# The low half of z made once per chunk and kept in DRAM; the down bias copied into the bank by ScalarE

## The reference

```
layer 0, per batch:
  q, k, v = x @ Wq, x @ Wk, x @ Wv;  attn = softmax(q k^T * 512**-0.5)
  a   = attn @ v @ Wp + bp
  cms = gelu(a @ cW1 + cb1) @ cW2 + cb2 + onehot(target)
  mod = gelu([a, cms] @ mW1 + mb1) @ mW2 + mb2
  z   = clip(x + cms + mod, 0, 1)
layer 1, per batch, with the weights of the batch's role (3 roles):
  h = gelu(z @ W_down[role] + b_down[role])          512 -> 256
  y = z + h @ W_up[role] + b_up[role]                256 -> 512
  out = layernorm(y) * gamma[role] + beta[role]
```

## Time and profile before

| | |
|---|---|
| time of the profiled execution | 2032.4 us |
| its span | 2030.8 us |
| median of three runs | 2033.6 us |
| busy: TensorE, weight load, VectorE, ScalarE | 2005.9, 1670.6, 1391.9, 950.2 us |
| mean granted TensorE clock | 0.998 |
| DMA of the whole program | 193.8 MB |
| last stage | from 1895 us on |
| store of 1 MB of z from POOL's queue, issue to landing | 5.1 us (median) |
| load of 128 KB of z, issue to landing | 2.1 us (median) |
| first half of `output` on VectorE, L1411 | 0.42 us |
| one clip, L1446 or L1457 | 0.42 us |
| DMA rate from 1894 to 1906 us | 374 to 430 GB/s |

### The profile page before, as it was taken

The page is one execution under the profiler, slowest core; times in us unless marked ns, Lnnn a source line. Parts: engine busy times, 40 slices in busy tenths (PEclk is TensorE's granted clock), DMA queues, the critical chain, the costliest instruction groups (busy, mean ns, idle before and its releaser), DMA issues.

```text
span 2030.8 us, 28039 instructions
## 1 busy us (share of the span) xinstructions
PE 2005.9 (99%) x9371; PEld 1670.6 (82%) x9371; DVE 1391.9 (69%) x2601; ACT 950.2 (47%) x1977; POOL 107.4 (5%) x199
## 2 busy tenths in 40 slices
PE   8999999999999999999999999999999999999997
PEld 7888878888888888888888888888888888888896
DVE  6786786555777686556686786565686686654897
ACT  4754453433654454333564453343374454433564
POOL 0000000000000000000000000000000000000132
PEclk9999999999999999999999999999999999999999
DMA  4121233315111143125111232224311132222754
GB/s 167 32 63 42 75 123 109 94 52 202 63 52 63 52 145 109 50 90 206 65 53 48 68 116 97 89 94 152 118 35 60 53 114 99 94 74 75 247 162 116
DMA packets 113024, 193.79 MB, mean 95 GB/s; under 512 B 12393, under 2 KB 72050, under 8 KB 108404
## 3 DMA queue, kind: packets, MB, share of 16 engines
q1 hardware_dynamic: 98404, 128.42, 20.1%
q0 software_dynamic: 14400, 63.46, 8.9%
q10 hardware_dynamic: 80, 0.13, 0.0%
HBM read 148.71 MB, written 43.26 MB: 95 GB/s over the span
## 4 chain that ended last, share of the span: by engine, by line
PE 91%; DVE 5%; DMA 2%; issue 1%; SPq 1%; ACT 0%; DVEq 0%; POOL 0%; POOLq 0%
PE y L1712 16%; PE y L1714 15%; PE y L1713 15%; PE x L1712 13%; PE x L1714 13%; PE x L1713 13%; PE y L1801 1%; PE x L1826 1%; DVE w_lo L1145 1%; DMA bet<-beta 1%; DVE c_forms L1307 1%; DMA w_blocks<-w1m 1%; PE x L2062 1%; DVE f L1211 0%; PE y L1800 0%
## 5 line engine op out<-in xcount | busy, mean ns | idle before, releaser
L693 ACT CAST w_hi<-w_blocks 128x512 fp32r<-128x512 f32 (+1 forms) x464 | 231.4, 519 | 124.6 <-PE y L1714 83.7
L1145 DVE TENSOR_TENSOR w_lo<-w_blocks,w_hi 128x512 fp32r<-128x512 f32 (+1 forms) x464 | 249.9, 564 | 54.7 <-ACT w_hi L693 54.7
L1712 PE MATMUL x<-h_hi,w_hi 128*128 128x512 f32 x512 | 199.7, 390 | 0.0
L1712 PE MATMUL y<-h_hi,w_hi 128*128 128x512 f32 x512 | 199.4, 389 | 0.0
L1713 PE MATMUL x<-h_lo,w_hi 128*128 128x512 f32 x512 | 199.3, 389 | 0.0
L1713 PE MATMUL y<-h_lo,w_hi 128*128 128x512 f32 x512 | 199.2, 389 | 0.0
L1714 PE MATMUL y<-h_hi,w_lo 128*128 128x512 f32 x512 | 199.2, 389 | 0.0
L1714 PE MATMUL x<-h_hi,w_lo 128*128 128x512 f32 x512 | 199.2, 389 | 0.0
L1712 PE MATMUL y<-a_forms,w_hi 128*128 128x512 f32 x480 | 187.9, 391 | 2.1 <-DVE f L1248 2.0
L1714 PE MATMUL y<-a_forms,w_lo 128*128 128x512 f32 x480 | 186.9, 389 | 0.0
L1713 PE MATMUL y<-a_forms,w_hi 128*128 128x512 f32 x480 | 186.8, 389 | 0.0
(11 more groups left out here) (240 smaller groups left out, 4243.2 us busy)
## 6 DMA issues: line engine op xcount, KB each, us to landing
w_blocks<-w1m SPq DMA_DIRECT2D x128, 256.0 KB, 4.5
w_blocks<-w1c SPq DMA_DIRECT2D x64, 256.0 KB, 3.2
w_st<-w2c SPq DMA_DIRECT2D x64, 256.0 KB, 3.1
w_st<-w2m SPq DMA_DIRECT2D x64, 256.0 KB, 4.7
x_hi_lo<-x_halves POOLq DMA_DIRECT2D x6, 2048.0 KB, 11.0
zs<-z_by_batch SPq DMA_DIRECT2D x66, 128.0 KB, 2.1
cms<-f SPq DMA_DIRECT2D x32, 256.0 KB, 2.8
z_cms<-cms POOLq DMA_DIRECT2D x8, 1024.0 KB, 7.0
```

The source lines that it names most:

```text
L693: nc.scalar.copy(w1_hi[:, w % RING, cols], src).then_inc(w1_hi_s, 1)
L1145: nc.vector.tensor_tensor(w1_lo[:, w % RING, cols], src, f32(w1_hi[:, w % RING, cols]), ALU.subtract).then_inc(w1_lo_s, 1)
L1712: nc.tensor.matmul(ps, w[0], x[0], start=first, stop=False, skip_group_check=more)
```

## The change

In each chunk of 512 values of finished z (8 chunks per super-tile), ScalarE copies the high half into `pre_hi` and VectorE subtracts it from z and writes the low half, one word in four, so that in the tile a token's four chunks lie together ("by token"). That tile (`x_st`, in the last stage `zr` and `zc`) is stored beside z in `z_dram`, and each load of the last stage brings both. The stationary operand of the low x high product is then read out of the loaded slot with a step of four words, and the split of z on VectorE is gone. ScalarE's split keeps its work. The down bias is loaded to all partitions by one DMA, and ScalarE copies its row into the PSUM bank two pairs ahead; the products add to it. The bias matmul, its ones, its zeroed tile and its pass through DRAM are gone. VectorE's calls of `z_chunk_lo` stand in the turns where ScalarE's calls of `z_chunk_hi` stand.

```diff
-PRE_W = (1, 1, 1, 1, 1, 1, 1, 0)
+PRE_W = (1, 1, 1, 1, 1, 1, 0, 0)
...
-    z_dram = nc.dram_tensor("z_by_batch", (B, P, DC * S), F32).ap()
+    z_dram = nc.dram_tensor("z_and_low_half", (B, P, 2, DC * S), F32).ap()
...
-            z_hi, z_lo = hl("z", [P, 2, DC, P], at_l1)
-            brow = sb("brow", [P, R, KD], F32R, at_l1)
+            z_hi = sb("z_hi", [P, 2, DC, P], F32R, at_l1)
+
+            zs = sb("zs", [P, 4, 2, 2, DC * S], F32R, at_l1)
+            brow = sb("brow", [P, R, KD], on=at_l1)
...
+        def low_tile(s, t):
+            tile = x_st if s + 1 < NS else (zr, zc)[t]
+            return tile[:].rearrange("p c n -> p (c n)").rearrange("p (b s c) -> p b s c", b=BT, c=DC)
...
@@ sync: load_z @@
                 if n >= 4:
-                    sp.wait_ge(zl_s, n - 3)
+                    sp.wait_ge(d_mm, n - 3)
                     sp.wait_ge(zf_s, n - 3)
                 for k, b in enumerate(batches_):
-                    sp.dma_start(zs[:, slot, k, :, :].rearrange("p c s -> p (c s)"),
-                                 z_dram[bass.ds(b, 1)].rearrange("o p f -> (o p) f")).then_inc(zl[slot], 16)
+                    sp.dma_start(f32(zs[:, slot, :, k]),
+                                 z_dram[bass.ds(b, 1)].rearrange("o p h f -> (o p) h f")).then_inc(zl[slot], 16)
...
-            sp.wait_ge(brow_zero, 1)
-            sp.dma_start(f32(brow[0:2]).rearrange("p r n -> p (r n)"), bd_dram).then_inc(row_in, 16)
+            sp.dma_start(brow[:], bd.to_broadcast([P, R, KD])).then_inc(row_in, 16)
...
+                if m == 4 + DC:
+                    sp.wait_ge(zl_c, 2 * DC * NS - DC)
+                    store_z(NT - 2, zr, last_stored[0], 1)
...
+                if m == 6 + 2 * DC:
+                    sp.wait_ge(zl_c, 2 * DC * NS)
+                    store_z(NT - 1, zc, last_stored[1], 1)
...
@@ gpsimd, start of super-tile s @@
                 if s:
+                    pool.wait_ge(zl_c, 2 * DC * s - DC)
+                    store_z(2 * s - 2, x_st, zl_stored, 1)
                     pool.wait_ge(z2_ready, DC * s)
                     store_z(2 * s - 1, h1_tile, z2_stored)
+                    pool.wait_ge(zl_c, 2 * DC * s)
+                    store_z(2 * s - 1, x_st, zl_stored, 1)
...
-                    pass_down_bias(2 * DC * s + 2 * R)
...
-                    nc.gpsimd.memset(f32(brow[:]), 0.0).then_inc(brow_zero, 1)
...
@@ scalar: gelu_plain, form_a @@
+                    act.wait_ge(zl_c, 2 * DC * s)
...
+                if s and k == P6 and h == 0:
+                    act.wait_ge(zl_stored, 32 * s)
...
+            def z_chunk_hi(s, t, c):
+
+                n = 2 * DC * s + DC * t + c
+                act.wait_ge((z1_ready, z2_ready)[t], DC * s + c + 1)
+                if n % (2 * DC) == 0:
+                    act.wait_ge(pre_stored, 32 * (2 * DC * (s + 1) if s + 1 < NS else 2 * DC * s + 2 * R))
+                if n:
+                    act.wait_ge(zl_c, n)
+                nc.scalar.copy(pre_hi[:].rearrange("p (b s) -> p b s", b=BT), (zb1, zb2)[t][:, :, c, :]).then_inc(zh_c, 1)
...
@@ scalar: attention @@
                 query(s, DC + 2)
+                if s:
+                    z_chunk_hi(s - 1, 0, 0)
                 split_a(s, 7)
+                if s:
+                    z_chunk_hi(s - 1, 0, 1)
                 query(s, DC + 3)
                 split_v(m0)
+                if s:
+                    z_chunk_hi(s - 1, 0, 2)
...
+                    if s and p == 2:
+                        z_chunk_hi(s - 1, 1, 0)
                     normalise_p(m + 1)
                     split_v(m + 1)
+                    if s and p < 5 and p != 1:
+                        z_chunk_hi(s - 1, *((0, 3) if p == 0 else (1, p - 1)))
...
@@ scalar: last stage @@
-                src = zs[:, slot].rearrange("p k c s -> p c k s")
+                src = f32(zs[:, slot, 0]).rearrange("p k (c s) -> p c k s", c=DC)
...
+            def down_bias(n):
+                if n == 0:
+                    act.wait_ge(row_in, 16)
+                r = act.value_load(role_t[0:1, n:n + 1], min_val=0, max_val=R - 1)
+                if n < 2:
+                    act.wait_ge(part_s, 8 * NQ * NS - 3 + n)
+                else:
+                    act.wait_ge(hgelu_s, n - 1)
+                nc.scalar.copy(d_ps[n % 2][:, 0:KD], brow[:, bass.ds(r, 1), :].rearrange("p o n -> p (o n)")
+                               ).then_inc(bias_s, 1)
...
                     gelu_pair(n + 1, (u + 1) % 2)
+                    if n + 3 < NPAIR:
+                        down_bias(n + 3)
...
                 unit(n, n, n + 2 < NPAIR, n + 1 < NPAIR)
+                if 4 <= n < 4 + DC:
+                    z_chunk_hi(NS - 1, 0, n - 4)
+                elif 9 <= n < 9 + DC:
+                    z_chunk_hi(NS - 1, 1, n - 9)
...
@@ vector @@
+            def z_chunk_lo(s, t, c):
+
+                last, n = s + 1 == NS, 2 * DC * s + DC * t + c
+                if c == 0 and last:
+                    dve.wait_ge((z1_ready, z2_s)[t], DC * NS)
+                elif c == 0:
+                    dve.wait_ge(*((zl_stored, 32 * s + 16) if t else (prod[P6], (2 * NQ - 1) * (s + 1))))
+                dve.wait_ge(zh_c, n + 1)
+                nc.vector.tensor_tensor(low_tile(s, t)[:, :, :, c].bitcast(F32R), (zb1, zb2)[t][:, :, c, :],
+                                        batches(f32(pre_hi[:])), ALU.subtract).then_inc(zl_c, 1)
...
                 inverse(m0 + 1)
                 if s:
+                    z_chunk_lo(s - 1, 0, 0)
                     z2_sum(s - 1, 2)
                 query(s, DC + 3)
                 if s:
                     z2_sum(s - 1, 3)
+                    z_chunk_lo(s - 1, 0, 1)
                 split_v(m0)
+                if s:
+                    z_chunk_lo(s - 1, 0, 2)
...
-                if z:
-                    split_z(n + 2, u + 2)
...
@@ tensor: down @@
-                pe.wait_ge(zl_s, n + 1)
-                if n < 2:
-                    pe.wait_ge(part_s, 8 * NQ * NS - 3 + n)
+                pe.wait_ge(zh_s, n + 1)
+                pe.wait_ge(bias_s, n + 1)
                 ps = d_ps[u % 2][:, 0:KD]
-                nc.tensor.matmul(ps, ones2[:], rows(brow[:], r), start=True, stop=False)
+                low = zs[:, u % 4, 1].rearrange("p k (s c) -> p (k s) c", c=DC)
                 for k in range(DC):
                     w = [rows(half[:, :, k, :], r) for half in (wd_hi, wd_lo)]
-                    ins = mm3(ps, (z_hi[:, u % 2, k, :], z_lo[:, u % 2, k, :]), w, False, k == DC - 1)
+                    ins = mm3(ps, (z_hi[:, u % 2, k, :], low[:, :, k]), w, False, k == DC - 1, True)
```

More of the change, by code:

```diff
@@ L451, in _, with store_z @@
                             sp.dma_start(cf_dram[2 * s + 1, :, c, :], f2[:, c, :]).then_inc(c2_stored[c], 16)
-            def store_z(t, tile, stored):
-                sp.dma_start(z_dram[t * BT:(t + 1) * BT].rearrange("b p f -> p b f"),
+            def store_z(t, tile, stored, h=0):
+                sp.dma_start(z_dram[t * BT:(t + 1) * BT, :, h].rearrange("b p f -> p b f"),
                             tile[:].rearrange("p c n -> p (c n)").rearrange("p (b f) -> p b f", b=BT)
@@ L508, in _ @@
                 if m == 4 * UNROLL + 1:
-                    sp.wait_ge(last_stored[0], 16)
-                    sp.wait_ge(last_stored[1], 16)
+                    sp.wait_ge(last_stored[0], 32)
+                    sp.wait_ge(last_stored[1], 32)
                 unit(m, m, m + 6 < NPAIR)
@@ L558, in pass_x @@
                 pass_block(b, xT[t, :, c, :], x_dram[t, 0, :, c, :], x_dram[t, 1, :, c, :])
[L561 to L567, removed]
             def pass_up(b):
@@ L573, in pass_up, with store_z @@
                     pass_block(b + i, flat[:, cols], wu_dram[0, :, cols], wu_dram[1, :, cols])
-            def store_z(t, tile, stored):
-                pool.dma_start(z_dram[t * BT:(t + 1) * BT].rearrange("b p f -> p b f"),
+            def store_z(t, tile, stored, h=0):
+                pool.dma_start(z_dram[t * BT:(t + 1) * BT, :, h].rearrange("b p f -> p b f"),
                             tile[:].rearrange("p c n -> p (c n)").rearrange("p (b f) -> p b f", b=BT)
@@ L1009, in _ @@
             split_z(0, 0)
+            def down_bias(n):
[8 more added lines that the diff above has]
+                               ).then_inc(bias_s, 1)
+            down_bias(0)
+            down_bias(1)
             split_z(1, 1)
@@ L1023, in unit @@
                     gelu_pair(n + 1, (u + 1) % 2)
+                    if n + 3 < NPAIR:
+                        down_bias(n + 3)
             gelu_pair(0, 0)
+            down_bias(2)
             for n in range(2):
@@ L1047, in split_projection @@
                 nc.vector.tensor_tensor(lo, src, f32(hi), ALU.subtract).then_inc(qw_lo, 1)
-            nc.vector.memset(ones2f[:], 1.0).then_inc(ones_s, 1)
-            dve.wait_ge(ones_s, 1)
-            nc.vector.tensor_copy(ones2[:], ones2f[:]).then_inc(ones_s, 1)
             for k in range(DC):
```

(19 more changed lines are left out.)

17 lines of the change are left out of this document (6 added, 11 removed).

## The result

The changed kernel takes 2063.6 us (median of four runs, 2062.6 to 2064.9) against 2033.2 us (four runs): a ratio of 1.0151, 95% interval 1.0138 to 1.0163. The forecast was 2058 us. The profiled executions lie a little apart from the medians (2064.9 and 2032.4 us), so their spans, 2063.3 and 2030.8, differ by 32.5 us where the medians differ by 30.3.

What follows compares the result with a forecast made beforehand. TensorE was taken as the bound, with VectorE nearly as full in attention and bounding the last stage up to pair 12. Terms 13.9 + 3.8 + 6.1 + 0.4 = +24.2 on 2032.4 gave 2056.6, median 2058 us; range 2037 to 2068.

Steps and rivals of the forecast that it cites:

- the last 20 pairs: End of the last stage, bound by TensorE: 19 pairs each 0.32 us longer, +6.1 us.
- the start: Start of the last stage: 1.4 MB more ahead of beta's load, +0.4 us, between -0.5 and +3.5.
- the attentions: Attention of super-tiles 1 to 3: late VectorE makes TensorE lose 4.6 us in each, +13.9 us.
- the first parts: Each attention up to the split of P: TensorE loses 1.6 us at L = 1.14, nothing at L = 0.60.
- the second parts: Each attention's turns 2 to 4: TensorE loses 4L - 1.55 = 3.0 us, 0.85 with L = 0.60.
- L: VectorE's low-chunk subtraction, start to start: taken as 1.14 us, with 0.60 as the lower end.
- The weight load: In `down`, 4 of 12 loads per pair read with the 16-byte step: 4 x 0.11 = 0.44 us per pair.
- The bias: Last stage: dropping the bias matmul saves TensorE 0.12 us per pair; the transposes' 0.08 passes to the next product.
- The rival that ended faster: Whole kernel: steps are free and the transposes' 0.08 goes with the bias matmul, 3.39 per pair, 2028 us; chance 0.07.
- Pairs 2 to 11: Last stage: pairs of 3.91, 4.46 and 4.20 us, together 42.2 against 38.4, +3.8 us.
- The rival on the last stage's DMA: Last stage: 768 instead of 512 KB per pair, DMA share 0.78 at most; in the range, no chance of its own.
- Only TensorE pays: Whole kernel: the step slows only TensorE's weight loads, +9.8 us, 2043 us; chance 0.10.

Runs made afterwards that it cites:

- e1: Changed kernel with VectorE writing the low chunk in whole runs of 64 words, TensorE's step kept: 2060.3 us.
- e7: Changed kernel with the attentions' low-chunk subtraction cut to one column per batch instead of 64, waits and bytes kept: 2054.6 us.
- e8: Changed kernel with the attentions' low-chunk subtraction and ScalarE's copies both cut to one column per batch, waits and bytes kept: 2053.5 us.
- e4: Changed kernel with z loads bringing only the high half from pair 4 on: 2060.1 us.
- e5: Changed kernel with the store of each pair's second row block moved from SyncE's queue to GpSimd's: 2061.7 us.
- e6: Changed kernel with a batch's halves side by side in the load buffer, 128 runs of 2 KB instead of 256 of 1 KB: 2056.0 us.
- e2: Changed kernel with `down` reading 128 adjacent words as low weights, VectorE's step kept: 2063.0 us.

## Why the prediction was right, and where it wasn't

The likeliest case came true: slower, both engines pay, 2063.6 inside 2037 to 2068. But 24.2 us were worked out and 32.5 came. The miss lies in the last 20 pairs (6.1 us too little), where the doubts had gone to TensorE's load and the DMA engines and none to the queue, and in the start (4.1 too little), less 1.5 too much for the attentions. That the total stayed in the range owes something to luck: the range had room for dearer steps, and a queue that it didn't consider used that room.

**The low chunk's price** was taken at 1.14 us, the upper end, and is 0.90 to 0.92. The row chosen as the nearest (each element counted twice) was too dear by 0.23. The Trainium skill's Vector Engine (DVE) Microarchitecture Reference (5.2) speaks of 1.71 to 2.51 ns per column for a destination that hops each element; 0.91 us over 512 columns is 1.78. The trace agrees with its lower end: over the contiguous write the excess is 0.31 us, 0.61 ns per column. Its direction was right where the rows with gaps had suggested no surcharge.

**The attentions**: forecast 13.9, measured 12.4 for the stretch and 11.1 in the attentions themselves, and close for a mixed reason. Put the measured 0.91 into the forecast's own steps and the first parts give 3 x 0.9 (measured 3 x 1.1), the second parts 3 x (4 x 0.91 - 1.55) = 6.3 (measured 7.8), in all 9.0. How the loss grows with L was right: from 0.60 to 0.91 the steps give 2.2 us more per attention, and 2.2 lie between e1 and the changed kernel. What was too kind is the part that doesn't hang on L: with L at 0.60 the forecast allowed 2.55 us, and e1 lost 4.4. Of these 1.6 are ScalarE's copies. In the first part the forecast moved ScalarE's work by 0.6 us and found nothing lost at L = 0.60; there e1 and e7 both lose 0.32 us per attention, and e8 nothing. In the second part it didn't count the copy, and 0.2 us per attention belong to it. So too high an L and too kind a base partly cancelled. What TensorE then waited for is what the forecast named, `output` and the split of P (changed kernel, waits, 495 to 600 us, none of them before):

```profile
PEld x L1881 <- DVE pt_hi_lo L1443: 3.8, 4, 1.0
...
PE x L1881 <- DVE f L1457: 1.8, 3, 0.7
```

**The weight load**: 4 x 0.11 forecast, 0.11 to 0.12 measured; the pair of 3.91 was met to the digit in e4, e5 and e6 (77.3 to 77.4 us where 71.2 + 6.1 = 77.3 were forecast). The Trainium skill's SBUF — State Buffer (Door 1, the note on cachelines) could be read both ways; of its two readings the one that wants at least two accesses in a 16-byte line is borne out by both engines.

**The bias**: 0.12 per pair, and the transposes' 0.08 passed on, held. In the changed kernel the first product behind the transposes is followed after 0.21 us (1985.02 to 1985.23). The rival that ended faster fell on this and on the step.

**Pairs 2 to 11**: +3.8 forecast, +4.0 measured, but pair by pair it was less good. Of the pairs with a z2 sum and a chunk three took 4.50 to 4.51 where 4.46 was said, and the first 4.76. Pairs 2, 3 and 8, said to follow TensorE at 3.91, took 3.61, 3.61 and 3.33, and within 0.01 the same in e2, where TensorE's step is gone; pair 9 took 5.08 instead of 4.20. The errors cancelled, which is luck.

**The last 20 pairs**: +6.1 forecast, +12.2 measured. The step that failed is the sentence on `load_z` and `store_second`. It counted the new wait against 2.1 us of landing, and found 2.6 pairs of room, but never added up what SyncE itself does in a pair. The count was to be had from the trace of before: 3.46 of 3.59 us, so 0.13 of slack, where a load gets twice the runs. The two stores of low halves on SP were named as work and given no price. The rival on the last stage's DMA looked at the share of the DMA engines (0.78 at most; 0.67 was measured from 1967 to 2049 us), which was beside the point. e4, e5 and e6 show it.

**The start**: +0.4 forecast, up to +3.5 allowed, +4.5 measured. The failing step is "from 1882 to 1890 the DMA engines are under half busy, enough for most of it". The z loads did run where the engines had room (a share of 0.80 from 1896 to 1904 us), but what stands behind them in the queue, beta last, runs in engines that are full, as they were before the change (1.00 from 1892 to 1908). Seen from the first product of `down`, beta was issued 3.0 us ahead instead of 5.1 and landed after 16.6 us instead of 13.7, so 5 us later. The upper bound, all 1.4 MB at 400 GB/s, came nearest; what holds the landing back is argued and not shown.

The case "Only TensorE pays" would look refuted by the totals, as e2's edit moved the median by 0.6 us. That would be a false reading: TensorE's surcharge was real (3.47 us per pair without it, 3.91 with it) and lay under SyncE's cycle of 3.95.

## What to carry to other kernels

An engine that only issues DMAs has a cycle too: add up its register reads, issues and steps per iteration and set the sum beside the bound, above all where a transfer is split into more runs. Two prices that are nearly equal hide each other, so removing one of them proves nothing in the total; divide the span into stretches and read each edit in its own. Work moved from a late stage into an earlier one is free only if every engine that it passes has slack there, the copying engine as much as the computing one.

## What the runs showed of the hardware

- A load of 256 KB as 256 runs of 1 KB took SyncE 0.54 to 0.55 us to issue. The same 256 KB as 128 runs of 2 KB took 0.33 to 0.35 (two with the gap between them in 0.87, against 1.28), as 128 KB in 128 runs did before. So the issue time grew with the number of runs and not with the bytes.
- VectorE writing single fp32 words 16 bytes apart took 1.08 us for 512 columns, 0.68 in runs of 64 words (from start to start 0.91 and 0.60). A weight load reading 128 columns with that step took 310 ns, 195 with adjacent words.
- A batch number's register read on SyncE took 0.28 + 0.15 us in the chain, besides the steps between; three per pair are a third of its cycle of 3.95.
- With the second store on GpSimd's queue the program ended later: from the last `ht_lo` 14.4 and 14.7 us in three runs instead of 13.1 and 13.6.
